# A second norm whose token shift goes through SBUF by DMA, with new instruction orders on all engines

## The chip, the cores and the metric

The kernel runs on one core of a Trainium2 chip. The metric is the device time in microseconds of one execution, as the median of several. TensorE multiplies matrices into PSUM, VectorE and ScalarE work element by element on SBUF and PSUM, GpSimd on SBUF alone, and SyncE (SP) issues the DMAs. Each engine runs its own list of instructions in order; they meet only at semaphores.

## The reference, cut to what matters

`x` is 32 sequences of 128 tokens of 128 features. A cross-attention stage comes first, and then six layers:

```
shift_tokens(t): a, s = halves of the features; s is moved down by one token, the first row is zero
for i in range(6):
    x = attn_layer(shift_tokens(x), ...) + x     # 16 heads of 64, rotary, l2norm of q and k, window 32
    x = ffn_layer(shift_tokens(x), ...) + x
ffn_layer(x): xn = (x - mean) / sqrt(var + 1e-5) * g + b
              a, gate = halves of xn @ W1 + b1 ;  return a * gelu(gate) @ W2 + b2
```

The change is in the second `shift_tokens` of each layer, ahead of the mean and variance of `ffn_layer`. All is float32.

## The kernel before, in words

**Units and rotations.** A unit is one sequence in one layer, 192 in all (`UNITS`). On SBUF a unit's activations are 128 tokens (partitions) by 128 features. The cross-attention (`xslot`, first 340 us) is not touched. After it every engine has a function `slot(n, k)` whose last lines call its parts in a fixed order written out by hand; `slots` (L238) calls it for n from -2 to 196, the middle in a loop of two. In slot n the engine works on several units: z (n+1 or n+2), a (n), m (n-1), b (n-2), c (n-3), d (n-4) and f (n-5). `part(n, lag)` gives the unit, `count` the value that a semaphore has once a unit's step is done. A slot is called a rotation below.

**A unit's way.** The input is copied and transposed (`next_input` L478, `transpose_z` L1272, `copy_z` L649; the first token shift is made by copy_z, which writes half of the rows one column further). a: TensorE makes q and k in four projections `proj_qk(0..3)` and v in two, `proj_v(0..1)`, each 128x512 into bank 0 or 1 in turn; VectorE's `rotary(j)` (two instructions, ta and tb) and ScalarE's `square(j)` read each q/k bank, so that `proj_qk(2)` waits for rotary(0), `proj_qk(3)` for rotary(1), `proj_v(r)` for rotary(r+2); GpSimd's `add(j)` adds ta and tb. `sum_squares` (L967) makes the norms, root(0..3) on VectorE with `log_sum` and `inverse_root` on ScalarE the inverse roots, and GpSimd's `normalize(j)` applies them to unit m. b: `transpose_qk` into banks 4 and 5, `copy_T` out of them, `scores` into banks 2 and 3, `maximum`, `subtract`, `exponent`, `sum_rows`, `invert`, and GpSimd's `weigh`. c: `transpose_P`, `copy_PT`, `attend`, `copy_o`. The values were written to vt by `copy_v` and put into three overlapping windows, vs, by `shift_v` on SP (L317), six DMAs a unit.

**The second norm, unit d.** `attn_out` (L1251) multiplies by Wo into bank 7. `z_mid` (L902) adds the residual and writes zm. `shift_tokens` (L1263) multiplies zm's first half of the features with the identity and its second half with a shift matrix, into bank 6. `norm_stats`, `norm_aggr`, `norm_var` (L911 to L928) take mean and variance from bank 6, GpSimd's `norm_rstd` (L463) the inverse root, and `norm_apply` (L930) reads bank 6 again and writes zn. Then `transpose_zn`, `copy_zn`, `ffn_gate`, `gelu`, `ffn_a`, `gated`. Unit f: `ffn_out` and `z_out` (L894). GpSimd's `residual` (L470) adds b2 to zm for z_out.

**Layer changes.** SP loads the next layer's weights between its shift_v calls (L341 to L362): `load_qk`, `load_v`, `load_o` and `load_ffn` (L298), whose last DMA is b2r. Each waits until the last unit of the layer has used the old weights.

Of the kernel before, what the change touches and what calls it, by code (L numbers as in the profile page):

```python
# [77 lines left out]
def build(nc, x, ctx, deltas, mask, xWq, xWk, xWv, xWo, xtw, Wqkv, qs, ks, Wo, lng, lnb, W1, b1, W2, b2, consts, out):  # L78
    es = ExitStack()
    with es:  # L80
# [6 lines left out]
        def sem(name):  # L87
# [5 lines left out]
        shift = cst[:, C_SH:C_SH + 128]  # L93
# [39 lines left out]
        zm = sb("zm", [128, 2, E])  # L133
# [53 lines left out]
            "l_gb", "l_b2", "l_rot", "l_v0", "l_v1",  # L187
# [7 lines left out]
            "p_zT", "p_qk", "p_v", "p_tr", "p_S", "p_PT", "p_AV", "p_y", "p_zsh", "p_znT", "p_gate", "p_a", "p_y2",  # L195
# [70 lines left out]
        def _(sp):  # L266
# [59 lines left out]

            sp.dma_start(qks[:, 0, :], qs.rearrange("l d -> (l d)").partition_broadcast(128)).then_inc(s["l_qks"], 16)
# [3 lines left out]
            for b in range(B):  # L331
                if b >= 2:

                    sp.wait_ge(s["x_A1"], b - 1)
                sp.dma_start(ctxb[:, b % 2, :], ctx[b, :, :]).then_inc(s[f"l_ctx{b % 2}"], 16)
                if b == 1:
                    load_qk(0)
                    load_v(0)
                    load_o(0)
                    load_ffn(0)  # L340
            for layer in range(DEPTH):  # L341
# [29 lines left out]
        def _(pool):  # L371
# [3 lines left out]
            g.memset(vaug[:, :, :, :], 0.0).then_inc(s["u_vz"], 1)  # L375

# [58 lines left out]
            def slot(n, k):  # L435
# [34 lines left out]
                def residual():  # L470

                    if d_on:
# [3 lines left out]
                        g.tensor_tensor(zmb[:, pd, :], zm[:, pd, :], b2r[:, :], ALU.add).then_inc(s["g_zmb"], 1)  # L476
# [27 lines left out]
                add(3)  # L504
                weigh(1)
# [5 lines left out]
        def _(act):  # L511
# [84 lines left out]
            def slot(n, k):  # L596
# [122 lines left out]
                copy_o(0)  # L719
                copy_o(1)  # L720
# [6 lines left out]
        def _(dve):  # L727
# [123 lines left out]
            def slot(n, k):  # L851
                a, a_on = part(n, 0)
                m, m_on = part(n, 1)
                b, b_on = part(n, 2)
                d, d_on = part(n, 4)
                f, f_on = part(n, 5)
                pm, pb, pd, pf = (k - 1) % 2, k % 2, k % 2, (k - 5) % 2
# [44 lines left out]
                def z_mid():  # L902

                    if d_on:
                        wait(dve, "p_y", count(1, d, 1))
                        wait(dve, "p_zsh", count(1, d - 2, 1))
                        wait(dve, "g_zmb", count(1, d - 2, 1))
                        v_.tensor_tensor(zm[:, pd, :], bank[7][:, 384:512], z_sb[:, cols(d)], ALU.add)\  # L908
# [67 lines left out]
                def sum_rows():  # L976

                    if b_on:
                        wait(dve, "a_exp", count(1, b, 1))
                        v_.tensor_reduce(rs, P[:, pb, :].rearrange("p (h t) -> p h t", t=DH), AX.X, ALU.add)\  # L980
                            .then_inc(s["d_sum"], 1)

                def invert():

                    if b_on:
# [365 lines left out]
```

## Time and profile before

| | |
|---|---|
| median of 3 runs | 3379.66 us (3376.93 to 3380.09) |
| the profiled execution | 3372.05 us, its span 3370.2 us |
| busy: TensorE, VectorE, ScalarE, GpSimd | 3264.7, 2873.8, 2751.3, 2505.5 us |
| granted TensorE clock, mean | 0.991 |
| DMA | 175.94 MB, 52 GB/s |
| longest group of TensorE | the q and k projections, L1149, 1536 matmuls, 806.6 us |
| longest group of GpSimd | add, L452, 768 of 1.28 us each |

A busy time says how long an engine had an instruction in work. Matmuls are pipelined, so that their records overlap by a few tenths; a piece of the chain of waits counts only up to the start of the next. In the rows, PE is TensorE, PEld its load of the stationary operand, DVE is VectorE, ACT ScalarE, POOL GpSimd, SPq the queue of SyncE. Times of a timeline are from the span's start.

### The profile page before, as it was taken

The numbers are of one execution on the slowest core, as the hardware profiler recorded it, in microseconds if no ns is written. First come the engines' busy times: TensorE is split into PE (matmuls) and PEld (weight loads), VectorE is DVE, ScalarE is ACT, GpSimd is POOL, SyncE is SP. The second block draws the span as 40 slices with busy tenths as digits, with TensorE's granted clock in tenths as the row PEclk, the third lists the DMA queues.
The fourth block names the chain that finished last, engine by engine and source line by source line (L and its number), as shares of the span: only waits on it lengthen the run. The fifth ranks groups of instructions, "written<-read, shape, count | busy, mean of one in ns | idle before, by whom it ended". The sixth has DMA issues, their size and how long they took to land.

```text
span 3370.2 us, 170013 instructions
## 1 busy us (share of the span) xinstructions
PE 3264.7 (97%) x65892; PEld 2345.6 (70%) x65892; DVE 2873.8 (85%) x6037; ACT 2751.3 (82%) x5265; POOL 2505.5 (74%) x2703
## 2 busy tenths in 40 slices
PE   6998799999999999999999999999999999999997
PEld 3444477777777777777777777777777777777775
DVE  5888788888888888888888888888888888888885
ACT  3666788888888888888888888888888888888886
POOL 3554677777787777778777787877777787777773
PEclk9999999999999999999999999999999999999998
DMA  2000121112212122221212212122211112221212
GB/s 77 8 7 5 39 57 47 53 50 67 69 47 56 47 55 68 61 55 47 56 47 75 61 49 54 47 56 67 68 48 51 52 47 79 57 56 47 53 50 55
DMA packets 125541, 175.94 MB, mean 52 GB/s; under 512 B 26742, under 2 KB 49332, under 8 KB 124724
## 3 DMA queue, kind: packets, MB, share of 16 engines
q1 hardware_dynamic: 125492, 175.28, 19.4%
q8 instruction: 31, 0.51, 0.1%
q14 instruction: 18, 0.15, 0.0%
HBM read 21.32 MB, written 2.10 MB: 7 GB/s over the span
## 4 chain that ended last, share of the span: by engine, by line
PE 78%; POOL 10%; issue 7%; DMA 1%; DVE 1%; ACT 1%; SPq 1%; POOLq 0%; ACTq 0%; DVEq 0%
PE bank L1149 16%; PE bank L1259 9%; PE bank L1167 9%; PE bank L1159 8%; PE bank L1230 7%; PE bank L1214 6%; POOL qk L452 4%; POOL qk L461 4%; PE bank L1051 3%; PE bank L1293 3%; PE bank L1247 3%; PE bank L1301 3%; PE bank L1268 2%; PE bank L1206 2%; POOL P L490 1%
## 5 line engine op out<-in xcount | busy, mean ns | idle before, releaser
L452 POOL TENSOR_TENSOR qk<-ta,tb 128x512 f32<-128x512 f32 x768 | 982.6, 1280 | 13.0 <-DVE tb L872 13.0
L1149 PE MATMUL bank<-wqkv,zsT 128*128 128x512 f32 x1536 | 806.6, 607 | 6.9 <-ACT zsT L659 2.6
L461 POOL TENSOR_TENSOR qk<-qk,rn 128x512 f32<-128x512 f32 x768 | 795.6, 1048 | 0.0
L610 ACT ACTIVATE sq<-bank 128x512 f32<-128x512 f32 x768 | 461.1, 600 | 322.6 <-PE bank L1149 313.5
L490 POOL TENSOR_TENSOR P<-P,rowsum 128x512 f32<-128x512 f32 x384 | 401.3, 1045 | 375.2 <-DVE rowsum L988 375.2
L869 DVE TENSOR_TENSOR ta<-bank,rot 128x512 f32<-128x512 f32 x768 | 525.8, 685 | 26.7 <-ACT sq L610 11.4
L872 DVE TENSOR_TENSOR tb<-bank,rot 128x512 f32<-128x512 f32 x768 | 521.2, 679 | 0.0
L973 DVE TENSOR_REDUCE bank<-sq 128x32 f32<-128x2048 f32 x192 | 437.8, 2280 | 0.3
L1159 PE MATMUL bank<-wqkv,zsT 128*128 128x512 f32 x768 | 412.3, 619 | 5.4 <-DVE tb L872 5.4
L1259 PE MATMUL bank<-wo,oT 128*128 128x128 f32 x3072 | 393.9, 281 | 0.7 <-ACT oT L636 0.7
L1259 PEld LDWEIGHTS bank<-wo,oT 128*128 128x128 f32 x3072 | 357.3, 191 | 13.8 <-ACT oT L636 1.1
L1167 PEld LDWEIGHTS bank<-cst,qk 64*128 64x128 f32 x6144 | 222.1, 139 | 174.0 <-issue 151.1
L1149 PEld LDWEIGHTS bank<-wqkv,zsT 128*128 128x128 f32 x1536 | 257.2, 198 | 105.9 <-issue 96.3
L1230 PE MATMUL bank<-PT,vs 64*64 64x32 f32 (+1 forms) x18432 | 307.9, 220 | 0.4 <-ACT PT L645 0.4
L1230 PEld LDWEIGHTS bank<-PT,vs 64*64 64x64 f32 x18432 | 286.7, 135 | 30.8 <-issue 30.8
L467 POOL TENSOR_TENSOR rstd<-ve,half_neg 128x1 f32<-128x1 f32 x192 | 105.7, 550 | 263.4 <-DVE ve L928 263.4
L1214 PEld LDWEIGHTS bank<-kT,qT 64*32 64x32 f32 x24576 | 277.4, 105 | 16.2 <-issue 5.9
L1214 PE MATMUL bank<-kT,qT 64*32 64x64 f32 x24576 | 281.0, 225 | 5.3 <-issue 5.3
L908 DVE TENSOR_TENSOR zm<-bank,z_sb 128x128 f32<-128x128 f32 x192 | 56.0, 291 | 263.4 <-PE bank L1259 263.4
L1167 PE MATMUL bank<-cst,qk 64*128 64x64 f32 x6144 | 274.4, 229 | 4.4 <-ACT oT L636 2.5
L620 ACT ACTIVATE qT<-bank 128x512 f32<-128x512 f32 x384 | 229.1, 597 | 47.7 <-PE bank L1167 47.7
L951 DVE TENSOR_TENSOR P<-bank,rowmax 128x512 f32<-128x512 f32 x384 | 260.0, 677 | 0.0
(133 smaller groups left out, 6298.3 us busy)
## 6 DMA issues: line engine op xcount, KB each, us to landing
vs<-vt SPq DMA_DIRECT2D x1152, 128.0 KB, 2.4
wqkv<-L_ffn_Wqkv SPq DMA_DIRECT2D x6, 1024.0 KB, 5.1
wqkv<-L_ffn_Wqkv SPq DMA_DIRECT2D x6, 512.0 KB, 3.8
wo<-L_ffn_Wo SPq DMA_DIRECT2D x6, 512.0 KB, 3.7
z_sb<-x SPq DMA_DIRECT2D x4, 512.0 KB, 6.9
ctxb<-ctx SPq DMA_DIRECT2D x32, 64.0 KB, 1.7
out<-x_sb SPq DMA_DIRECT2D x8, 256.0 KB, 3.5
w<-L_ffn_W SPq DMA_DIRECT2D x6, 341.0 KB, 3.1
```

The source lines that it names most:

```text
L452: g.tensor_tensor(o, i0, i1, ALU.add).then_inc(s["g_add"], 1)
L461: g.tensor_tensor(q3, q3, r3, ALU.mult).then_inc(s["g_qk"], 1)
L610: a_.activation(sq[:, 512 * j:512 * j + 512], bank[j % 2][:, :], ACT.Square)\
L869: v_.tensor_tensor(ta[:, c].rearrange("p (h d) -> p h d", d=DH), bank[j % 2][:, :].rearrange("p (h d) -> p h d", d=DH), rot[:, o:o + 64].u ...
L872: v_.tensor_tensor(tb[:, c].rearrange("p (h c d) -> p h c d", c=2, d=32)[:, :, ::-1, :], bank[j % 2][:, :].rearrange("p (h c d) -> p h c d ...
L973: v_.tensor_reduce(sm, sq[:, :].rearrange("p (h d) -> p h d", d=DH), AX.X, ALU.add)\
L1149: t_.matmul(bank[j % 2][:, :], zsT[:, k % 2, :], wqkv[:, 512 * j:512 * j + 512], start=True, stop=True).then_inc(s["p_qk"], 1)
L1159: t_.matmul(bank[r][:, :], zsT[:, k % 2, :], wv[:, :, r, :], start=True, stop=True)\
L1167: ins = t_.transpose(bank[4 + t][:, 64 * p:64 * p + 64], src[tok, 128 * p:128 * p + 128], ident[tok, tok])
L1214: ins = t_.matmul(SC[e][32 * w:32 * w + 32, 64 * p:64 * p + 64], qT2[dr, p, 32 * w:32 * w + 32], kT2[dr, p, k0:k0 + 64], start=False, stop ...
L1230: ins = t_.matmul(bank[4 + r][64 * e:64 * e + 64, 128 * i + q0:128 * i + q0 + nq], vs[kr, pc, w, hc:hc + 64], PT[kr, 4 * e + i, q0:q0 + nq ...
L1259: ins = t_.matmul(bank[7][:, 384:512], oT[:, p, :], wo[:, 2 * (p % 4) + p // 4, :], start=p == 0, stop=p == PAIRS - 1)
```

## The change

It does four things.

1. `zm` has three parts of 64 features: part 0 the first half, part 2 the second half, part 1 the second half one token later. z_mid writes parts 0 and 2. Row 0 of part 1 is set to zero once by GpSimd.
2. `shift_tokens` on TensorE is gone. SP's new `shift_z` copies part 2 of rows 0 to 126 to part 1 of rows 1 to 127 by one DMA. norm_stats waits for it, and norm_stats and norm_apply read parts 0 and 1 in SBUF. SP issues shift_z(u) ahead of shift_v(u + 3); at a layer change it stands between the loads.
3. sum_rows and invert work on unit n-3 in place of n-2, so that they stand at the start of the next rotation. attend waits for its values itself; values_here is gone.
4. The orders in `slot` of TensorE, VectorE, ScalarE and GpSimd are new.

```diff
-        zm = sb("zm", [128, 2, E])
+        zm = sb("zm", [128, 2, 3, E // 2])
...
@@ SP
+            def shift_z(u, par):
+                wait(sp, "d_zm", count(1, u, 1))
+                sp.dma_start(zm[1:128, par, 1, :], zm[0:127, par, 2, :]).then_inc(s[f"l_s{par}"], 16)
...
                 with sp.Fori(0, (B - 6) // 2) as i:
                     for k in range(2):
+                        shift_z(i * 2 + (start + k), k)
                         shift_v(i * 2 + (start + 3 + k), (3 + k) % 2)
+                shift_z(end - 6, 0)
                 shift_v(end - 3, 1)
+                shift_z(end - 5, 1)
                 if layer + 1 < DEPTH:
                     load_qk(layer + 1)
                 shift_v(end - 2, 0)
                 if layer + 1 < DEPTH:
                     load_v(layer + 1)
+                shift_z(end - 4, 0)
                 shift_v(end - 1, 1)
+                shift_z(end - 3, 1)
                 if layer + 1 < DEPTH:
                     shift_v(end, 0)
+                shift_z(end - 2, 0)
+                if layer + 1 < DEPTH:
                     shift_v(end + 1, 1)
                     load_o(layer + 1)
+                shift_z(end - 1, 1)
+                if layer + 1 < DEPTH:
                     shift_v(end + 2, 0)
                     load_ffn(layer + 1)
@@ GpSimd
+            g.memset(zm[:, :, 1, :], 0.0).then_inc(s["u_s0"], 1)
...
+                next_input()
+                add(0)
                 norm_rstd()
+                normalize(0)
                 residual()
-                add(0)
-                normalize(0)
                 normalize(1)
                 add(1)
+                add(2)
                 normalize(2)
-                next_input()
                 normalize(3)
-                add(2)
                 weigh(0)
+                weigh(1)
                 add(3)
-                weigh(1)
@@ ScalarE
                 square(0)
                 copy_T(0)
+                copy_T(1)
+                square(1)
                 log_sum()
-                copy_T(1)
                 inverse_root()
-                square(1)
                 copy_T(2)
                 copy_T(3)
                 square(2)
-                act.preload_act_table_set("gelu_and_others")
                 copy_z()
                 copy_PT(0)
+                copy_PT(1)
+                square(3)
+                act.preload_act_table_set("gelu_and_others")
                 copy_zn()
-                square(3)
-                copy_PT(1)
+                copy_o(0)
+                copy_o(1)
                 copy_v(0)
                 gelu()
                 act.preload_act_table_set("natural_log_exp_and_others")
                 exponent()
-                copy_o(0)
-                copy_o(1)
                 copy_v(1)
@@ VectorE
                 def norm_stats():
-                        wait(dve, "p_zsh", count(1, d, 1))
-                        v_.bn_stats(stats[:, 0:6], bank[6][:, 0:128]).then_inc(s["d_bn"], 1)
+                        wait(dve, f"l_s{pd}", ...)
+                        v_.bn_stats(stats[:, 0:6], zm[:, pd, 0:2, :].rearrange("p c e -> p (c e)"))
...
-                        v_.tensor_scalar(zn[:, :], bank[6][:, 0:128], mv[:, 0:1], rstd[:, pd:pd + 1],
+                        v_.tensor_scalar(zn[:, :], zm[:, pd, 0:2, :].rearrange("p c e -> p (c e)"), mv[:, 0:1], ...
...
new order: root(0) sum_rows z_mid invert rotary(0) rotary(1) root(1) root(2) root(3) rotary(2)
           norm_stats norm_aggr norm_var z_out maximum(0) norm_apply rotary(3) maximum(1)
           subtract(0) subtract(1) sum_squares gated
@@ TensorE
                 def attend():
-                        pe.wait_ge(s["l_wv"], 16)
+                        wait(pe, f"l_v{pc}", ...)
                         wait(pe, "a_PT", count(2, c, 2))
+                        pe.nop(nofuse=True)
                 def attn_out():
-                        edge(pe, n, "a_gelu", count(1, d - 1, 1))
+                        wait(pe, "a_gelu", count(1, d - 1, 1))
...
                 proj_qk(0)
-                ffn_out()
                 transpose_qk(0)
                 attn_out()
                 proj_qk(1)
                 transpose_qk(1)
-                shift_tokens()
+                ffn_out()
                 proj_qk(2)
                 transpose_z()
+                proj_qk(3)
                 transpose_P()
                 scores()
+                attend()
                 transpose_zn()
-                proj_qk(3)
-                values_here()
                 proj_v(0)
                 ffn_gate()
+                proj_v(1)
                 ffn_a()
-                attend()
-                proj_v(1)
```

## Rows read from the trace of the kernel before

**Rows 1.** The page: busy time, share of the span, instructions; the chain by engine.

```profile
PE 3264.7 (97%) x65892; PEld 2345.6 (70%) x65892; DVE 2873.8 (85%) x6037; ACT 2751.3 (82%) x5265; POOL 2505.5 (74%) x2703
...
PE 78%; POOL 10%; issue 7%; DMA 1%; DVE 1%; ACT 1%; SPq 1%; POOLq 0%; ACTq 0%; DVEq 0%
```

**Rows 2.** The chain of one rotation: start in us, its share in us, what.

```profile
1500.72 0.11 PE bank L1278
1500.83 0.64 PE bank L1167 x16
...
1503.09 0.26 PE bank L1284
1503.35 0.86 PE bank L1149 x2
...
1506.39 1.53 PE bank L1230 x96
1507.93 1.05 PE bank L1159 x2
...
1509.84 0.67 PE bank L1247 x6
...
1514.64 0.36 PE bank L1268 x2
...
1515.23 0.98 PE bank L1149 x2
```

**Rows 3.** The chain from 860 to 1360 us: two starts of attn_out, 11 rotations apart.

```profile
937.68 1.98 PE bank L1259 x16
...
1107.80 1.98 PE bank L1259 x16
```

**Rows 4.** Timeline of VectorE: start, us, instruction, idle before it and its releaser.

```profile
1514.35 0.68 DVE L872 TENSOR_TENSOR tb<-bank,rot 128x512 f32<-128x512 f32 x1
...
1517.28 0.40 DVE L935 TENSOR_SCALAR zn<-bank,mv,rstd 128x128 f32<-128x128 f32 x1
1517.59 0.68 DVE L869 TENSOR_TENSOR ta<-bank,rot 128x512 f32<-128x512 f32 x1
...
1518.79 1.28 DVE L942 TENSOR_REDUCE rowmax<-bank 128x8 f32<-128x512 f32 x2
...
1525.35 1.21 DVE L980 TENSOR_REDUCE bank<-P 128x16 f32<-128x1024 f32 x1
...
1527.01 0.19 DVE L882 TENSOR_SCALAR bank<-bank 128x32 f32<-128x32 f32 x1
1528.86 0.29 DVE L908 TENSOR_TENSOR zm<-bank,z_sb 128x128 f32<-128x128 f32 x1 [1.67 <-PE bank L1259]
1529.19 0.69 DVE L869 TENSOR_TENSOR ta<-bank,rot 128x512 f32<-128x512 f32 x1
```

**Rows 5.** Norm instructions from SBUF, cross-attention part; last, norm_rstd later; durations ns min/median/max.

```profile
L842 DVE TENSOR_SCALAR z_sb<-x1cur,mv,rstd x32: 346/1051/1056, 62.3 to 340.0; 128x128 f32 x26, 128x128 f32<-128x128 f32 x6
...
199.42 1.04 POOL L416 TENSOR_TENSOR qk<-qk,xmax 128x512 f32<-128x512 f32 x1
199.49 1.05 DVE L842 TENSOR_SCALAR z_sb<-x1cur,mv,rstd 128x128 f32 x1 [0.30 <-POOL rstd L428]
...
207.25 0.28 DVE L825 BATCH_NORM_STATS2 stats<-x1cur 128x6 f32<-128x128 f32 x1
...
1516.12 0.55 POOL L467 TENSOR_TENSOR rstd<-ve,half_neg 128x1 f32<-128x1 f32 x1 [1.38 <-DVE ve L928]
```

**Rows 6.** shift_v's DMAs, 860 to 1360 us: issue in ns, landing, min/median/max.

```profile
L325 SPq DMA_DIRECT2D vs<-vt x193: 461/597/614, 859.8 to 1356.0; - x193
...
DMA to landing us min/median/max: 2.2/2.4/2.5
```

**Rows 7.** Timeline of SP at a layer change: first and last DMA of load_ffn.

```profile
891.47 0.53 SPq L304 DMA_DIRECT2D gb<-L_ffn_ln_g  x1
...
896.82 0.34 SPq L315 DMA_DIRECT2D b2r<-L_ffn_b  x1
```

More of the change, by code:

```diff
@@ L475, in residual @@
                         wait(pool, "z_ready", count(1, d - 2, 1) + B if not (isinstance(d, int) and d < 2) else 0)
-                        g.tensor_tensor(zmb[:, pd, :], zm[:, pd, :], b2r[:, :], ALU.add).then_inc(s["g_zmb"], 1)
+                        g.tensor_tensor(zmb[:, pd, :].rearrange("p (c e) -> p c e", c=2), zm[:, pd, 0:3:2, :],
+                                        b2r[:, :].rearrange("p (c e) -> p c e", c=2), ALU.add)\
+                            .then_inc(s["g_zmb"], 1)
                 def next_input():
@@ L854, in slot @@
                 b, b_on = part(n, 2)
+                c, c_on = part(n, 3)
                 d, d_on = part(n, 4)
                 f, f_on = part(n, 5)
-                pm, pb, pd, pf = (k - 1) % 2, k % 2, k % 2, (k - 5) % 2
+                pm, pb, pc, pd, pf = (k - 1) % 2, k % 2, (k - 3) % 2, k % 2, (k - 5) % 2
                 ym, sm, n0, n1, rs = rn[:, pm, :], SC[0][:, 0:32], SC[0][:, 32:64], SC[0][:, 64:96], SC[1][:, 0:16]
@@ L905, in z_mid @@
                         wait(dve, "p_y", count(1, d, 1))
-                        wait(dve, "p_zsh", count(1, d - 2, 1))
                         wait(dve, "g_zmb", count(1, d - 2, 1))
-                        v_.tensor_tensor(zm[:, pd, :], bank[7][:, 384:512], z_sb[:, cols(d)], ALU.add)\
+                        v_.tensor_tensor(zm[:, pd, 0:3:2, :], bank[7][:, 384:512].rearrange("p (c e) -> p c e", c=2),
+                                         z_sb[:, cols(d)].rearrange("p (c e) -> p c e", c=2), ALU.add)\
                             .then_inc(s["d_zm"], 1)
@@ L913, in norm_stats @@
                     if d_on:
-                        wait(dve, "p_zsh", count(1, d, 1))
-                        v_.bn_stats(stats[:, 0:6], bank[6][:, 0:128]).then_inc(s["d_bn"], 1)
+                        wait(dve, f"l_s{pd}", 16 * (d // 2) + 16 if isinstance(d, int) else (d >> 1) * 16 + 16)
+                        v_.bn_stats(stats[:, 0:6], zm[:, pd, 0:2, :].rearrange("p c e -> p (c e)"))\
+                            .then_inc(s["d_bn"], 1)
                 def norm_aggr():
@@ L976, in sum_rows @@
                 def sum_rows():
-                    if b_on:
-                        wait(dve, "a_exp", count(1, b, 1))
-                        v_.tensor_reduce(rs, P[:, pb, :].rearrange("p (h t) -> p h t", t=DH), AX.X, ALU.add)\
+                    if c_on:
+                        wait(dve, "a_exp", count(1, c, 1))
+                        v_.tensor_reduce(rs, P[:, pc, :].rearrange("p (h t) -> p h t", t=DH), AX.X, ALU.add)\
                             .then_inc(s["d_sum"], 1)
                 def invert():
-                    if b_on:
-                        wait(dve, "d_sum", count(1, b, 1))
-                        wait(dve, "g_P", count(2, b - 1, 2))
+                    if c_on:
+                        wait(dve, "d_sum", count(1, c, 1))
+                        wait(dve, "g_P", count(2, c - 1, 2))
                         v_.reciprocal(rowsum[:, :], rs).then_inc(s["d_rec"], 1)
-                z_out()
-                root(0)
-                z_mid()
-                rotary(0)
-                root(1)
-                norm_stats()
-                root(2)
-                norm_aggr()
-                root(3)
-                norm_var()
-                rotary(1)
+                root(0)
+                sum_rows()
+                z_mid()
+                invert()
+                rotary(0)
+                rotary(1)
+                root(1)
+                root(2)
+                root(3)
+                rotary(2)
+                norm_stats()
+                norm_aggr()
+                norm_var()
+                z_out()
+                maximum(0)
                 norm_apply()
-                rotary(2)
-                maximum(0)
+                rotary(3)
                 maximum(1)
                 subtract(0)
-                rotary(3)
                 subtract(1)
+                sum_squares()
                 gated()
-                sum_squares()
-                sum_rows()
-                invert()
             slots(dve, slot)
@@ L1221, in attend @@
                     if c_on:
-                        pe.wait_ge(s["l_wv"], 16)
+                        wait(pe, f"l_v{pc}", 96 * (c // 2) + 96 if isinstance(c, int) else (c >> 1) * 96 + 96)
                         wait(pe, "a_PT", count(2, c, 2))
+                        pe.nop(nofuse=True)
                         for i in range(4):
@@ L1234, in attend @@
                                 ins.then_inc(s["p_AV"], 1)
-                def values_here():
-                    if c_on:
-                        wait(pe, f"l_v{pc}", 96 * (c // 2) + 96 if isinstance(c, int) else (c >> 1) * 96 + 96)
                 def ffn_out():
@@ L1261, in attn_out @@
                         ins.then_inc(s["p_y"], 1)
-                def shift_tokens():
-                    if d_on:
-                        wait(pe, "d_zm", count(1, d, 1))
-                        wait(pe, "z_ready", (count(1, f, 1) if isinstance(f, int) else d) + B)
-                        t_.matmul(bank[6][:, 0:64], ident, zm[:, pd, 0:64], start=True, stop=True)
-                        t_.matmul(bank[6][:, 64:128], shift, zm[:, pd, 64:128], start=True, stop=True)\
-                            .then_inc(s["p_zsh"], 1)
                 def transpose_z():
```

8 lines of the change are left out of this document (5 added, 3 removed).

## The prediction

> **What bounds the kernel now.** I read the page's busy times first, then the chain that ended last, then one rotation of that chain piece by piece, then the timeline of the other engines over the same rotation. TensorE is busy for 97% of the span, VectorE for 85%, and TensorE holds 78% of the chain [rows 1]. The word "rotation" below is one call of `slot`: one unit enters and the engines work on units n to n-5. In the steady part the chain is TensorE without a break: the 11 rotations between the two starts of attn_out take 170.12 us, so one takes 15.465 us [rows 3]. Its pieces are one 512-column projection at 0.86 us, a group of 16 transposes at 0.64, attend at 1.53, and so on [rows 2]. VectorE sat idle for 1.67 us in that rotation, just ahead of z_mid, which waits for attn_out [rows 4]. So work taken from TensorE pays until another loop closes at its own length; how much pays is the question.
>
> **What goes from TensorE.** The two matmuls of shift_tokens hold the chain from 1514.64 to 1515.23, 0.59 us [rows 2]. The order also drops one change of operand shape from 64-row groups to 128 rows. What such a change costs: proj_v(1) behind attend takes 1.05 against 0.86 (0.19) and proj_qk(2) behind the shift 0.98 against 0.86, which is partly its wait for rotary(0) [rows 2]. In the new order proj_v(1) and proj_qk(2) have 128-row work ahead of them (-0.19, -0.12), ffn_out gets such a change in their place (+0.17, my value between 0 and 0.19), and transpose_zn keeps its 0.26 behind attend in place of the scores. TensorE alone would come to 15.465 - 0.59 - 0.19 - 0.12 + 0.17 = 14.74 us.
>
> **The loop that closes first.** z_mid now is followed by invert, rotary(0) and rotary(1), and proj_qk(3) waits for rotary(1), since it takes bank 1 (`d_rot` of j - 1). Counted from z_mid's start: z_mid to the next operation 0.33, invert about 0.17 (as the short operations, 0.19 long and overlapping), rotary(0) 1.20 by the distance of two VectorE operations around a rotary, then rotary(1)'s second half ends 0.60 + 0.68 later: 2.98 us [rows 4]. From the end of a rotary's second half (1514.35 + 0.68 = 1515.03) to the end of the projection that waited for it (1515.23 + 0.98 = 1516.21) is 1.18 us [rows 2, 4]. So proj_qk(3) ends 4.16 us after z_mid starts. z_mid starts about 0.23 behind attn_out's end, an estimate somewhat under the 0.32 that the hand-over from VectorE to TensorE costs (1.18 - 0.86); I use it again for maximum(0) behind the scores. In the same time TensorE has only proj_qk(1) 0.86, transpose_qk(1) 0.64, ffn_out 0.84, proj_qk(2) 0.86, transpose_z 0.11, proj_qk(3) 0.86 = 4.17 us of work [rows 2] where the path by VectorE takes 4.39: TensorE stalls by 0.2 in each rotation. That makes 14.74 + 0.22 = 14.96 us.
>
> VectorE has a loop of the same length. Behind proj_qk(3): transpose_P 0.64, masks and scores 1.62 (from the end of the transposes at 1501.47 to 1503.09), 0.23 of latency [rows 2]: maximum(0) starts 6.65 us after z_mid. From there to sum_rows VectorE does what it did before from norm_apply to sum_rows (1517.28 to 1525.35, 8.07 us), less rotary(2) (1.20) and with root(0) (0.17): 7.04; sum_rows 1.21; and z_mid again [rows 4]. That is 14.90 us, and about 0.1 for subtract(1), whose whole 0.68 the sum of squares must now await where gated() stood between: 15.0 us. VectorE's own work fits in (its idle time is now ahead of maximum(0), 0.6 to 0.9 us). ScalarE's work is unchanged: 82% of 15.465 is 12.7 us [rows 1], which leaves it over 2 us of 15.0. I cost its new order at nothing; what it could delay is transpose_qk(1), which needs banks 4 and 5 back from copy_T(1), and each tenth by which copy_T(1) were late there would be a tenth per rotation. GpSimd has the same instructions as before; weigh waits for invert, which is behind z_mid now, but transpose_P has 3.5 us more of TensorE work ahead of it than the two weighs' 2.1 (two of 1.04 us, the form and length of [rows 5]).
>
> **The transfer.** shift_z is one DMA per unit, waited for three rotaries and three roots later. Between z_mid's end and norm_stats lie invert, 3 x 1.20 and the dependent roots, some 4.5 us. No transfer of this shape (127 partitions of 256 bytes, inside SBUF) is in the trace. The nearest, vs<-vt inside SBUF, lands 2.2 to 2.5 us after its issue, and an issue holds SP for 0.46 to 0.61 us [rows 6]. Bounds: 2.2 and, with an issue ahead of it, 3.1; I take 2.4 and so nothing in the steady rotations. SP has the six issues of shift_v behind it, not ahead of it: 7 x 0.65 = 4.6 us of a rotation.
>
> **norm_stats and norm_apply read SBUF now.** bn_stats from SBUF took 0.28 in the cross-attention part against 0.30 from PSUM: nothing [rows 5]. The tensor_scalar is another matter. From PSUM it took 0.40 [rows 4]. The same operation from SBUF to SBUF took 1.05 us when a GpSimd tensor_tensor had begun 0.07 us before it, ending 0.08 us after that one (199.42 + 1.04 and 199.49 + 1.05), and 0.346 at the shortest of 32 [rows 5]. So the price is from -0.05 to +0.65 us per rotation, somewhat more behind a longer GpSimd instruction. It depends on the phase. GpSimd's norm_rstd waits for norm_var (it did so before, 1.38 us [rows 5]), so normalize(0) starts about 0.6 us after it, near 6.4 us (statistics from 4.9, the three dependent steps 0.9), and holds until 7.4; norm_apply comes at 6.65 + 0.60 = 7.25. It would end near 7.6, as from PSUM. I take +0.1 for the spread: 15.1 us per rotation.
>
> The Trainium skill (SBUF — State Buffer, on the shared port pair) says that a VectorE instruction in a 2-port mode and a GpSimd instruction take an exclusive lock: the later one "fully blocks". The trace's 1.05 us row agrees with it. By that rule the sum is 15.0 or 15.65 us a rotation, as the phase has it; that is the second rival below.
>
> **Layer changes.** load_ffn(layer + 1) stands ahead of the next layer's first shift_z on SP. It begins when gated() of the last unit is done, about 13.7 us after z_mid, and its issues took 5.35 us up to b2r's [rows 7]. So shift_z of the new layer's first unit is issued about 19.6 us after the z_mid before (z_mid's own time is 15.1), lands at 22.0 to 22.3, where norm_stats would stand at 19.9. Of the 2.2 us the idle time ahead of maximum(0) takes 0.6: 1.7 us at each of 5 changes, +9 us (bounds 0 and 15). Before, a late b2r held only GpSimd there.
>
> **The tail.** In the last rotations nothing covers the transfer: 2.4 and an issue's 0.5 in place of TensorE's 0.59 and its hand-over of 0.3, about +2 us in each of three, +6.
>
> **Sum.** About 188 full rotations x (15.1 - 15.465) = -68.6; +9; +6: -54 us. The profiled execution took 3372.05 us (span 3370.2, 1.85 around it): 3318. The median of the runs shown is 7.6 above that execution, so about 3326.
>
> **The rivals.**
> 1. TensorE stays the only bound, the latencies that I added between engines being too long by 0.2 us. For it: its chain had no gap before. Against: the loop by rotary(1) is two rows long and not a guess. 188 x (14.74 - 15.465) = -136, +15: 3258 in this state of the count. 16%.
> 2. The other side: norm_apply is caught by a GpSimd instruction in most rotations. Place: VectorE's loop, which has nothing to give between maximum(0) and z_mid, and transpose_zn, which waits for it with 0.3 us in hand. Price 0.65: 15.0 + 0.65 = 15.65, 188 x 0.185 = +35, +15: 3430. It turns the change into a loss from 0.39 us per rotation on (15.465 - 15.0 - 15/188 = 0.385). For it: with a median of 1.051 over 32 at least half were caught there [rows 5], and GpSimd is busy 74% of the span [rows 1]. Against: the phase above. 14%.
> 3. The transfer lands behind norm_stats' place, because shift_v's issues get ahead of it: 3.9 us of issues, 6.3 us, 1.8 late, of which 0.7 is idle time anyway: +1.1 on 15.1 for all rotations, 3326 + 207 = 3533. Against: the order on SP, where both values' semaphores are up before z_mid's. 4%.
> 4. One engine's new order makes a loop of about the old length (a copy_T(1) that transpose_qk(1) awaits, an exponent that sum_rows awaits: both have 0.1 to 0.3 us in hand) and nothing moves: 3380. 6%.
>
> **Chances.** The forecast has 60%, with 3290 to 3360 as its own range (0.2 us of a rotation is 38 us). About 0.2% is what a measurement of this kernel can tell from no change. Faster: the 60 and 16, and 1 from the mild form of the second: 0.77. Same: 4's 6%, 0.06. Slower: 13 of the second and 4 of the third, 0.17. The range reaches to the first rival's value, 3258, and over the mild half of the second: 3258 to 3405.
>
> **What would show it.** A distance of attn_out's starts of 15.0 to 15.2 us. Idle time of TensorE's weight load for rotary(1) ahead of proj_qk(3), 0.1 to 0.3 us in each rotation. zn's tensor_scalar at 0.35 to 0.7 us; at 1.0 and above the second rival holds. No VectorE wait for the DMA in steady rotations and one of 1.5 to 3 us at each of 5 layer changes. Distances of 14.7 would show the first rival; a wait for zm's DMA in all rotations the third; 15.4 or more without either the fourth.

## The result: 0.5% faster, a third of the gain forecast, and the profile after

| | before | after |
|---|---|---|
| median of 7 runs | 3379.66 us (3371.06 to 3381.19) | 3360.43 us (3353.22 to 3364.67) |
| ratio | | 0.9947, 95% interval 0.9935 to 0.9958 |
| profiled execution, its span | 3372.05, 3370.2 us | 3357.84, 3356.0 us |
| one rotation, mean of 16 (distance of z_mid's starts) | 15.466 us | 15.186 us |

The forecast was 3326 us, -54; measured are -19 between the medians and -14.2 between the two spans. The page's busy times and its chain by engine, after, beside [rows 1]:

```profile
PE 3232.1 (96%) x65124; PEld 2208.1 (66%) x65124; DVE 2921.4 (87%) x6037; ACT 2673.6 (80%) x5265; POOL 2501.8 (75%) x2704
...
PE 90%; issue 3%; DVE 3%; DMA 1%; POOL 1%; ACT 1%; SPq 1%; DVEq 0%; ACTq 0%; POOLq 0%
```

TensorE is busy 32.6 us less. What that bought is seen in the chain of one rotation (start, share in us, what), which answers to [rows 2]; L1170 is proj_qk, L1188 a group of transposes, L1264 ffn_out, L1286 transpose_z, L1180 proj_v, L1301 ffn_gate, L1309 ffn_a, L1276 attn_out:

```profile
1509.21 0.65 PE bank L1188 x16
1509.85 0.86 PE bank L1264 x6
1510.72 1.00 PE bank L1170 x2
1511.72 0.11 PE bank L1286
1511.83 1.09 PE bank L1170 x2
...
1517.84 0.79 PE bank L1301 x6
1518.63 0.86 PE bank L1180 x2
1519.49 0.66 PE bank L1309 x6
```

The matmuls of the shift and the dearer proj_v are gone. But proj_qk(2) takes 1.00 and proj_qk(3) 1.09 where 0.86 is the work, and ffn_gate 0.79 where the like-sized ffn_a takes 0.66: TensorE waits in three places. VectorE and SP over the same rotation, from the timeline (start, us, instruction, idle before it and its releaser), beside [rows 4]:

```profile
1508.74 0.29 DVE L927 TENSOR_TENSOR zm<-bank,z_sb 128x128 f32<-128x128 f32 x1 [0.47 <-PE bank L1276]
1509.06 0.64 SPq L329 DMA_DIRECT2D zm<-zm  x1
...
1511.05 0.68 DVE L892 TENSOR_TENSOR tb<-bank,rot 128x512 f32<-128x512 f32 x1
...
1513.68 0.28 DVE L935 BATCH_NORM_STATS2 stats<-zm 128x6 f32<-128x128 f32 x1
```

z_mid still waits for attn_out (0.47 us), and proj_qk(3) begins as rotary(1)'s second half ends (1511.05 + 0.68 = 1511.73): that is the loop of the forecast. The statistics need no wait for the transfer in this rotation.

Cut at z_mid's starts, the 14.2 us come out as follows. 191 rotations at -0.280 make -53.5. Five things give a part of it back. The first z_mid starts 2.6 us later (398.16 against 395.53). The first four rotations stood 1.8 us above the mean before and stand 6.6 above it after: 4.8. The twelve rotations around each of the five layer changes stood 6.4 us above the mean in all and stand 24.2 above: 17.8. The last six were 7.6 us under the mean and are 4.2 over it: 11.7. Behind the last z_mid 22.0 us follow in place of 19.8: 2.2. The sum is -14.4.

The first of the five is not the change's. The cross-attention stage, which is the same in both kernels, already ran 5.0 us late at its first norm and 5.7 at its last in this one execution of the changed kernel; the line of [rows 5] reads 62.3 to 340.0 before and here:

```profile
L861 DVE TENSOR_SCALAR z_sb<-x1cur,mv,rstd x32: 347/1051/1056, 67.3 to 345.7; 128x128 f32 x26, 128x128 f32<-128x128 f32 x6
```

In the profiled executions of the experiments its last norm starts anywhere from 339.2 to 351.0. From there to the first z_mid the changed kernel takes 52.5 us, the kernel before 55.5. Without this scatter the two spans differ by 20 us, as the medians do.

### The profile page after: what moved, and what is told of

It reads as the page before. It is cut to its first block, busy times and chain, and to the rows that moved or that the text cites. A ratio compares the mean times of both kernels' runs of the same rounds, so it can differ in the third digit from the quotient of the medians.

```text
span 3356.0 us, 168541 instructions
## 1 busy us (share of the span) xinstructions
PE 3232.1 (96%) x65124; PEld 2208.1 (66%) x65124; DVE 2921.4 (87%) x6037; ACT 2673.6 (80%) x5265; POOL 2501.8 (75%) x2704
## 2 busy tenths in 40 slices
DMA packets 150118, 182.19 MB, mean 54 GB/s; under 512 B 51318, under 2 KB 73908, under 8 KB 149300
## 4 chain that ended last, share of the span: by engine, by line
PE 90%; issue 3%; DVE 3%; DMA 1%; POOL 1%; ACT 1%; SPq 1%; DVEq 0%; ACTq 0%; POOLq 0%
PE bank L1170 20%; PE bank L1276 11%; PE bank L1188 10%; PE bank L1180 9%; PE bank L1252 8%; PE bank L1235 7%; PE bank L1264 5%; PE bank L1301 4%; PE bank L1309 4%; PE bank L1072 3%; PE bank L1227 2%; PE bank L1292 1%; PE bank L1089 1%; DMA zm<-zm 1%; PE bank L1286 1%
## 5 line engine op out<-in xcount | busy, mean ns | idle before, releaser
L469 POOL TENSOR_TENSOR qk<-ta,tb 128x512 f32<-128x512 f32 x768 | 969.0, 1273 | 10.4 <-DVE tb L892 10.4
L1170 PE MATMUL bank<-wqkv,zsT 128*128 128x512 f32 x1536 | 818.8, 615 | 4.9 <-DVE tb L892 2.2
L509 POOL TENSOR_TENSOR P<-P,rowsum 128x512 f32<-128x512 f32 x384 | 392.4, 1042 | 514.8 <-DVE rowsum L1009 514.8
L1188 PEld LDWEIGHTS bank<-cst,qk 64*128 64x128 f32 x6144 | 221.8, 139 | 291.5 <-issue 291.5
L1180 PE MATMUL bank<-wqkv,zsT 128*128 128x512 f32 x768 | 400.5, 604 | 2.4 <-DVE tb L892 2.3
L1276 PE MATMUL bank<-wo,oT 128*128 128x128 f32 x3072 | 395.4, 282 | 0.5 <-ACT gl L709 0.5
L1276 PEld LDWEIGHTS bank<-wo,oT 128*128 128x128 f32 x3072 | 358.9, 192 | 13.8 <-issue 0.9
L963 DVE TENSOR_REDUCE rowmax<-bank 128x8 f32<-128x512 f32 x384 | 263.1, 685 | 93.2 <-PE bank L1235 93.1
L664 ACT ACTIVATE PT<-bank 128x512 f32<-128x512 f32 x384 | 208.4, 595 | 159.1 <-PE bank L1188 159.1
L1170 PEld LDWEIGHTS bank<-wqkv,zsT 128*128 128x128 f32 x1536 | 232.3, 191 | 110.9 <-DVE tb L892 98.0
L1188 PE MATMUL bank<-cst,qk 64*128 64x64 f32 x6144 | 274.3, 229 | 2.5 <-issue 2.1
## 6 DMA issues: line engine op xcount, KB each, us to landing
zm<-zm SPq DMA_DIRECT2D x192, 31.8 KB
```

Source lines behind the costliest of these rows:

```text
L469: g.tensor_tensor(o, i0, i1, ALU.add).then_inc(s["g_add"], 1)
L1170: t_.matmul(bank[j % 2][:, :], zsT[:, k % 2, :], wqkv[:, 512 * j:512 * j + 512], start=True, stop=True).then_inc(s["p_qk"], 1)
L1180: t_.matmul(bank[r][:, :], zsT[:, k % 2, :], wv[:, :, r, :], start=True, stop=True)\
L1188: ins = t_.transpose(bank[4 + t][:, 64 * p:64 * p + 64], src[tok, 128 * p:128 * p + 128], ident[tok, tok])
L1276: ins = t_.matmul(bank[7][:, 384:512], oT[:, p, :], wo[:, 2 * (p % 4) + p // 4, :], start=p == 0, stop=p == PAIRS - 1)
```

## Experiments

Ratios are to the kernel before, timed in the same batches. "Rotation" is the mean of 16; "changes" the excess over the mean of the five layer changes. Diffs are against the changed kernel, that of e9 against e5, those of e10 and e11 against e9.

| kernel | edit | ratio, 95% | rotation | changes |
|---|---|---|---|---|
| after | | 0.9947, 0.9935 to 0.9958 | 15.186 | 24.2 |
| e3 | new orders, shift on TensorE | 0.9966, 0.9949 to 0.9982 | 15.367 | 0.3 |
| e1 | SP's order | 0.9884, 0.9859 to 0.9909 | 15.189 | 1.0 |
| e2 | invert ahead of z_mid | 0.9932, 0.9908 to 0.9955 | 15.166 | 30.2 |
| e4 | ffn_gate later | 0.9963, 0.9947 to 0.9979 | 15.213 | |
| e7 | rotary(0), invert ahead of z_mid | 0.9942, 0.9927 to 0.9958 | 15.183 | |
| e5 | e7 and e1 | 0.9890, 0.9870 to 0.9909 | 15.192 | 8.9 |
| e8 | old orders, transfer | 1.1443, 1.1422 to 1.1464 | 17.834 | |
| e6 | GpSimd's phase | 0.9991, 0.9979 to 1.0004 | 15.244 | |
| e9 | e5, GpSimd waits for norm_apply | 0.9747, 0.9723 to 0.9771 | 14.927 | 9.1 |
| e10 | e9, z_mid earlier | 0.9756, 0.9732 to 0.9781 | 14.929 | |
| e11 | e9, another tail | 0.9776, 0.9753 to 0.9798 | 14.93 | |

**e3: the orders without the transfer.** The shift is back on TensorE, between ffn_out and proj_qk(2).

```diff
-        zm = sb("zm", [128, 2, 3, E // 2])
+        zm = sb("zm", [128, 2, E])
...
                 ffn_out()
+                shift_tokens()
                 proj_qk(2)
```

> The new orders on all engines, with the second norm's token shift back on TensorE (two matmul groups between ffn_out and proj_qk(2)) and no transfer of zm. Theory A (a rotation closes by z_mid, invert, rotary(0), rotary(1), proj_qk(3) and TensorE's chain behind it): the shift puts 0.59 us into the stretch of TensorE between attn_out and proj_qk(3), which has 0.2 to 0.35 us to give, so a rotation is 14.9 (TensorE alone with its wait for copy_zn) + 0.6 = 15.5 us; the layer changes, the start and the tail lose nothing to a transfer: about 3375 us, ratio 0.995 to 1.005, so the orders alone bring nothing. Theory B (VectorE with its 90% busy time is the bound, TensorE only follows): a rotation stays at 15.19 and the time falls to about 3325 us, ratio 0.984.

The orders alone bring 15.466 to 15.367, the transfer the next 0.18. The chain of e3; L1265 and L1266 are the two groups of the shift, L1150 proj_qk(2) and (3):

```profile
1521.08 0.17 PE bank L1265 x2
1521.25 0.22 PE bank L1266 x2
1521.47 0.91 PE bank L1150 x2
...
1522.50 0.86 PE bank L1150 x2
```

Behind 128-row work the shift costs 0.39 us, not the 0.59 of [rows 2], and proj_qk(3) does not wait. So the transfer takes 0.39 off TensorE and gives 0.21 of it back as waits. It also owns the layer changes (0.3 us here against 24.2): over 191 rotations its 0.18 is 34 us, and the changes eat 24 of them. I had expected 15.5 us and no gain from the orders, with the shift at 0.59. The last six rotations take 95.49 us here, 95.30 after and 85.24 before. The lost tail therefore belongs to the orders.

**e1: SP's order.** shift_z(end - 1) goes ahead of load_o and the new layer's first shift_z ahead of load_ffn.

```diff
-                shift_z(i * 2 + (start + k), k)
                 shift_v(i * 2 + (start + 3 + k), (3 + k) % 2)
+                shift_z(i * 2 + (start + 1 + k), (1 + k) % 2)
...
-                    load_o(layer + 1)
                 shift_z(end - 1, 1)
                 if layer + 1 < DEPTH:
+                    load_o(layer + 1)
                     shift_v(end + 2, 0)
+                    shift_z(end, 0)
                     load_ffn(layer + 1)
```

> The changed kernel with another order on SP at the layer changes alone: shift_z(end - 1) ahead of load_o, and shift_z of the next layer's first unit ahead of load_ffn. Theory A (the uncovered transfers of zm cost 3.3 to 5.5 us at each of 5 layer changes, since they queue behind wo's 512 KB and behind load_ffn's twelve issues): the rotation at a layer change falls from 18.3 to 20.7 us to 15.2 to 16 us, all others stay at 15.12 and 15.26, and the time falls by 17 to 24 us, to about 3340, ratio 0.987 to 0.990. Rival (the loss there is from the weights' own arrival, b2r and w1, as it was before the change): less than 5 us, since these DMAs now come 1 us later.

The excess of 24.2 falls to 1.0 and the ratio by 0.0063, 21 us, with the same rotation. The loss at the changes is thereby shown to be SP's order. In the timeline of the changed kernel at one change, the transfer of the layer's last unit is issued behind the 512 KB of wo, and that of the next unit behind load_ffn's issues:

```profile
875.25 0.39 SPq L295 DMA_DIRECT2D wo<-L_ffn_Wo  x1
875.76 0.66 SPq L329 DMA_DIRECT2D zm<-zm  x1
...
880.93 0.29 DVE L935 BATCH_NORM_STATS2 stats<-zm 128x6 f32<-128x128 f32 x1 [0.52 <-DMA zm<-zm]
...
890.85 0.29 DVE L927 TENSOR_TENSOR zm<-bank,z_sb 128x128 f32<-128x128 f32 x1
...
895.38 0.67 SPq L329 DMA_DIRECT2D zm<-zm  x1
...
899.40 0.29 DVE L935 BATCH_NORM_STATS2 stats<-zm 128x6 f32<-128x128 f32 x1 [3.53 <-DMA zm<-zm]
```

The first transfer is a piece of 5.14 us in the chain. The second is issued 4.2 us after its z_mid has ended, and the statistics wait 3.53. e1 moved both at once; the distances of z_mid's starts part them. In the rotation of the first transfer they are 15.26 to 15.42 us at the five changes, 15.26 in e1; in that of the second 18.33 to 20.68, against 15.12. So nearly all is lost behind load_ffn. The first adds to it by making gated, and with it load_ffn, 0.3 to 0.6 us later.

More is lost there than the wait. norm_apply, now in the time of a GpSimd instruction, takes 0.81 us, and TensorE stands 2.7 to 3.5 us without work ahead of transpose_zn. At four of the five changes its granted clock fell in this idle time or just behind it from 1.00, the upper level (2.4 GHz), to 0.50, the lower one (1.2 GHz), for some 3 to 7 us, and one or both proj_v took up to twice their time. At the change near 1882 us the clock stayed at 1.00 behind a like idle time (2.90). The first three lines are TensorE's idle time (timeline), its clock (a stretch of 2 us, third figure from the end) and proj_v(1) (chain) at the first change; the last is proj_v(1) near 1882 us:

```profile
901.94 0.33 PE L1292 MATMUL bank<-cst,zn 128*128 128x128 f32 x1 [2.91 <-DVE zn L956]
904.00:906.00 2.00, 2.00 (x5) 0.97 (x4) 1.87 (x3) 1.98 (x5) 2.00 (x3) 0.50 0.04 12
904.35 1.71 PE bank L1180 x2
...
1886.51 0.86 PE bank L1180 x2
```

The rotation with the clock at 1.00 throughout took 18.33 us, the four others 19.84 to 20.68: 1.5 to 2.4 us more, some 7 of the 24 us in all. That is an estimate, since the waits differ too (3.2 to 4.1).

In e1 the issues stand the other way round, and the statistics start without a wait. A late arrival of the new weights, the other reading of the change's cost, is thereby refuted: they are issued later in e1, behind the transfer.

```profile
893.64 0.66 SPq L329 DMA_DIRECT2D zm<-zm  x1
894.40 0.79 SPq L303 DMA_DIRECT2D gb<-L_ffn_ln_g  x1
...
898.26 0.28 DVE L936 BATCH_NORM_STATS2 stats<-zm 128x6 f32<-128x128 f32 x1
```

**e2: invert ahead of z_mid.**

```diff
                 sum_rows()
-                z_mid()
                 invert()
+                z_mid()
                 rotary(0)
```

> The changed kernel with invert ahead of z_mid on VectorE, where VectorE has 0.3 to 0.5 us of idle time, in place of behind it. Theory A (the path by z_mid, invert, rotary(0) and rotary(1) holds proj_qk(3)): the path shortens by 0.18 us, a rotation comes to 15.0 to 15.05 us, TensorE's wait for rotary(1) nearly goes, and the time falls by some 30 us to 3330, ratio 0.985. Theory B (VectorE's own work is the bound): the same instructions, no change, 0.9947. Theory C (TensorE with its wait ahead of ffn_gate is the bound already): no change either, and its wait ahead of proj_qk(3) turns into another.

It should shorten the loop by rotary(1), and the rotation moves by 0.02. VectorE's timeline in e2 shows why:

```profile
1511.36 1.21 DVE L1001 TENSOR_REDUCE bank<-P 128x16 f32<-128x1024 f32 x1
1512.73 0.26 DVE L1009 RECIPROCAL rowsum<-bank 128x16 f32<-128x16 f32 x1 [0.15 <-DVE bank L1001]
1513.13 0.29 DVE L927 TENSOR_TENSOR zm<-bank,z_sb 128x128 f32<-128x128 f32 x1
```

Right behind its source the reciprocal starts 1.37 us after sum_rows, z_mid 0.40 after that, and z_mid has no wait for attn_out left: VectorE's own chain has taken over at nearly the same length.

**e4: ffn_gate behind proj_v(1)**, to cover its wait for copy_zn.

```diff
                 proj_v(0)
-                ffn_gate()
                 proj_v(1)
+                ffn_gate()
```

> The changed kernel with proj_v(1) ahead of ffn_gate on TensorE. In the changed kernel ffn_gate's first matmul group takes 0.79 us of the chain in place of 0.66, since only proj_v(0) stands between transpose_zn and it while copy_zn runs. Theory A: those 0.13 us per rotation go, a rotation is 15.05 us, the time falls by 20 to 25 us, ratio 0.988. Rival (gelu and with it the exponent come 0.4 us later on ScalarE, so that sum_rows and z_mid on VectorE wait): 0 to 0.1 us per rotation worse, ratio 0.995 to 1.0.

Nothing is gained (15.213, 0.03 more). In e4's chain the wait reappears as a piece without work ahead of transpose_qk(1), which needs the banks of copy_T(1):

```profile
1506.10 0.32 issue
1506.42 0.71 PE bank L1188 x16
```

ScalarE's copy_T(0) and copy_T(1) run from 1505.23 to 1506.32 there, ending 0.1 us ahead of that group: with gelu later, ScalarE works without a pause from gelu to copy_T(1), and its loop closes at about the old length.

**e7 and e5: rotary(0) first.** e7 takes z_mid out of the path to rotary(1); e5 adds e1's edit.

```diff
                 sum_rows()
-                z_mid()
-                invert()
                 rotary(0)
+                invert()
+                z_mid()
                 rotary(1)
```

> The changed kernel with VectorE's order root(0), sum_rows, rotary(0), invert, z_mid, rotary(1) in place of root(0), sum_rows, z_mid, invert, rotary(0), rotary(1). Rotary(0) then fills the time in which VectorE waits for attn_out, and only rotary(1) stands behind z_mid. Theory A' (invert's move brought nothing because a reciprocal right behind its reduction stalls and z_mid then starts late by VectorE; proj_qk(3) does wait for rotary(1)): rotary(1) ends some 0.4 to 0.5 us sooner, TensorE's 0.2 to 0.4 us ahead of proj_qk(2) and proj_qk(3) go, a rotation comes to 14.9 to 15.0 us, about 3315 us, ratio 0.982. Theory C (TensorE's own chain is at its end in the changed kernel, whatever VectorE does): 15.15 to 15.19, no change. Risk: one rotary less covers the transfer; it lands 3.1 us after z_mid's end at a place that now is 3.3 to 3.7 us behind it.

> The same VectorE order together with the SP order that was tried by itself (shift_z(end - 1) ahead of load_o, the next layer's first shift_z ahead of load_ffn). Theory A': the two gains add, since they lie in different rotations: about 3295 us, ratio 0.976. If VectorE's order brings nothing: 3340, 0.988.

The rotation stays at 15.18. The timeline of e7:

```profile
1505.51 0.29 DVE L935 BATCH_NORM_STATS2 stats<-zm 128x6 f32<-128x128 f32 x1 [0.31 <-DMA zm<-zm]
...
1506.94 1.04 POOL L478 TENSOR_TENSOR qk<-qk,rn 128x512 f32<-128x512 f32 x1
1507.19 0.87 DVE L956 TENSOR_SCALAR zn<-zm,mv,rstd 128x128 f32<-128x128 f32 x1
1508.12 0.33 PE L1292 MATMUL bank<-cst,zn 128*128 128x128 f32 x1 [0.16 <-DVE zn L956]
```

z_mid no longer waits for attn_out; it starts 1.6 us behind it. The loop is now VectorE's own, through the transfer: VectorE waits for the landing (0.31), and between the statistics and the next z_mid it never stands idle for longer than 0.13. In that stretch lies norm_apply, which begins inside GpSimd's normalize(0), ends 0.08 us after it, takes 0.87 us in place of 0.34, and now makes TensorE wait. Both are terms of this loop; e9 takes out the second.

**e8: the transfer alone**, in the old orders.

> The kernel before with only the token shift by the transfer inside SBUF (zm's three parts, shift_z on SP, no shift_tokens on TensorE), all orders on TensorE, VectorE, ScalarE and GpSimd as before. Between z_mid and norm_stats lie only rotary(0) and root(1), 1.5 us, and the transfer needs about 3: VectorE waits some 1.6 us in every rotation. Theory A (TensorE waits for rotary(1), which is behind norm_stats here): a rotation grows to 15.8 to 16.3 us, 3440 to 3540 us, ratio 1.02 to 1.05. Rival (the wait only takes the place of VectorE's idle time ahead of z_mid, 1.0 to 1.7 us a rotation): no change or the 0.4 us gained from TensorE, ratio 0.98 to 1.0.

The ratio was far above the 1.02 to 1.05 that I expected: the price is 2.37 us per rotation. Its timeline:

```profile
1510.03 0.29 DVE L926 TENSOR_TENSOR zm<-bank,z_sb 128x128 f32<-128x128 f32 x1 [0.52 <-PE bank L1279]
1510.35 0.64 SPq L329 DMA_DIRECT2D zm<-zm  x1
...
1514.05 0.29 DVE L934 BATCH_NORM_STATS2 stats<-zm 128x6 f32<-128x128 f32 x1 [2.25 <-DMA zm<-zm]
...
1516.06 1.12 DVE L955 TENSOR_SCALAR zn<-zm,mv,rstd 128x128 f32<-128x128 f32 x1
```

VectorE stands 2.25 us for the transfer, and norm_apply takes 1.12 us where it took 0.40 [rows 4]. The transfer is issued 0.03 us after z_mid's end, so nothing on SP holds it up. The three rotaries and three roots that the new orders put between are a condition of the transfer.

**e6: GpSimd's phase.** residual ahead of normalize(0).

```diff
                 norm_rstd()
-                normalize(0)
                 residual()
+                normalize(0)
```

> The changed kernel with residual ahead of normalize(0) on GpSimd, both behind norm_rstd. normalize(0) then starts 0.4 us later, still runs when norm_apply comes, and ends 0.4 us later. Theory A (the two-port read of zm waits until the GpSimd instruction that holds the port is done, so only the phase made it cheap): norm_apply takes 0.7 to 0.8 us in the steady rotations in place of 0.34, and as VectorE has only 0.3 to 0.5 us to give ahead of z_mid, a rotation grows by 0 to 0.15 us, ratio 0.995 to 1.002. Rival (0.34 is what this instruction takes beside GpSimd in any phase): 0.34, and 0.9947.

All norm_apply of the changed kernel, of e6, of e7 and of e9, one line each (ns min/median/max):

```profile
L956 DVE TENSOR_SCALAR zn<-zm,mv,rstd x192: 336/339/934, 405.0 to 3339.4; 128x128 f32<-128x128 f32 x192
```

```profile
L956 DVE TENSOR_SCALAR zn<-zm,mv,rstd x192: 336/733/1241, 397.9 to 3344.1; 128x128 f32<-128x128 f32 x192
```

```profile
L956 DVE TENSOR_SCALAR zn<-zm,mv,rstd x192: 403/880/1437, 399.0 to 3335.0; 128x128 f32<-128x128 f32 x192
```

```profile
L959 DVE TENSOR_SCALAR zn<-zm,mv,rstd x192: 335/338/470, 399.2 to 3270.1; 128x128 f32<-128x128 f32 x192
```

Moving a small GpSimd instruction takes it from 0.34 to 0.73 us, and the rotation grows by 0.06; the other 0.3 us were in hand. So the second rival's mechanism is real; in the changed kernel the phase avoids it. The Trainium skill (SBUF — State Buffer, Who interferes with whom) says that the later of the two is fully blocked. e6 and e7 agree: in e6 normalize(0) starts at 1510.21 and takes 1.05 us, norm_apply starts at 1510.59 and ends at 1511.34, 0.1 behind it, as in e7.

**e9: e5, and GpSimd's normalize(0) waits for norm_apply.**

```diff
                         wait(pool, "g_add", count(4, m, j + 1))
+                        if j == 0 and d_on:
+                            wait(pool, "d_zn", count(1, d, 1))
```

> The kernel with rotary(0) ahead of z_mid and the two shift_z ahead of the weights' loads, plus one wait: GpSimd's normalize(0) waits for d_zn, so that norm_apply reads zm with GpSimd quiet. In the run without that wait norm_apply took 0.87 us and TensorE waited 0.16 us for it in each rotation. Theory A'' (what held the rotation at 15.19 there was norm_apply behind normalize(0), 0.53 us on VectorE's chain, in place of the path by rotary(1)): norm_apply 0.34 us, a rotation of 14.9 to 15.0 us, about 3290 to 3300 us, ratio 0.976 to 0.978. Rival (the transfer of zm, awaited 0.3 us in each rotation there, or TensorE's own chain holds it): 15.1 to 15.19, ratio 0.986 to 0.989. GpSimd has 3.0 us of idle time per rotation for the wait.

This is the fastest kernel: 0.9747, 3288.55 us. Against e5 the rotation falls by 0.265 us; over 191 rotations that is 51 us, and the ratios differ by 0.0143, 48 us. Every norm_apply now runs free, and e9's chain has proj_qk(2) and proj_qk(3) at 0.86 (L1173), with ffn_gate's wait alone left (L1304):

```profile
1508.48 0.86 PE bank L1173 x2
...
1509.45 0.86 PE bank L1173 x2
...
1515.23 0.80 PE bank L1304 x6
```

GpSimd pays for it where hardly anybody waits. In the waits of 1000 to 3300 us (sum, count, longest) it idles 145.9 us for norm_apply, 1 us a rotation:

```profile
POOL qk L481 <- DVE zn L959: 145.9, 149, 2.7
```

At the layer changes 9 us stay in e5 and e9 where e1 has 1.0. GpSimd's residual waits for b2r there, up to 4.4 us; that this is the cause was not tried.

**e10: e9 with z_mid ahead of invert**, 0.2 us earlier against attn_out.

```diff
                 rotary(0)
-                invert()
                 z_mid()
+                invert()
                 rotary(1)
```

> The same with z_mid ahead of invert behind rotary(0), which issues the transfer 0.17 us sooner and weigh later. If the wait for the transfer holds the rotation: 0.1 to 0.17 us less per rotation, 20 to 30 us less than the kernel with invert first. If TensorE's chain or another loop does: the same within 0.2%.

The same within the interval (14.929). In e9 the landing is no longer a bound: TensorE's own chain is. In e7 and e5 it is another matter. The statistics waited for it in about 140 of 151 rotations there, in 8 in e9. That the lock on norm_apply held them is shown by e9; whether an earlier landing would have helped them as well was not tried.

**e11: another tail.** In the last five rotations of e9, TensorE puts attend behind ffn_a, where it stood in the kernel before, and leaves out the projections, which have no unit left; ScalarE puts gelu and exponent ahead of copy_o.

```diff
+                if isinstance(n, int) and n >= UNITS:
...
+                    scores()
+                    transpose_zn()
+                    ffn_gate()
+                    ffn_a()
+                    attend()
...
```

> The fastest kernel so far (rotary(0) first, shift_z ahead of the weights, normalize(0) awaiting d_zn) with the order of before in the last five rotations alone (n from UNITS on) on TensorE and ScalarE: attend behind ffn_a in place of ahead of transpose_zn, and gelu and exponent ahead of copy_o. Theory T (the tail's loss of 11 to 12 us in the changed kernel is from the orders, since attend stands ahead of transpose_zn there and with no projections to hide it the norm's chain waits for it; the kernel with the orders alone and no transfer lost 11 of them too): 4 to 10 us less in the last six rotations, about 3282 us, ratio 0.972 to 0.9735. Rival (the tail's loss is the uncovered transfer, 3.5 to 3.7 us a unit): the last six rotations as long as before, no change.

The last six rotations take 98.94 us against 94.53 in e9. My reading of the tail fell. By e3 its loss lies in the orders; which of them stays open.

## Why the prediction was wrong: the loop named rightly, four terms too small

Of the 39 us between the forecast's -54 and the -14 of the two spans, 15 lie in the steady rotations, 9 at the layer changes, 7 at the start (5.7 of them the scatter told above, -3.1 and +4.8 the change's) and 8 in the tail.

**The steady rotation** was forecast at 15.1 and measured at 15.186, a fall of 0.280 where 0.365 was forecast. The loop that closes first is the one named: z_mid, rotary(0), rotary(1), proj_qk(3), with a stall of 0.23 and 0.16 in two rotations running where 0.2 was forecast. The waits of the changed kernel from 1000 to 3300 us (about 151 rotations; sum, count, longest) say the same, and name the other two places:

```profile
PEld bank L1170 <- DVE tb L892: 72.1, 149, 0.5
PEld bank L1301 <- ACT znT L686: 103.2, 150, 0.8
...
DVE rowmax L963 <- PE bank L1235: 70.9, 144, 2.0
...
DVE stats L935 <- DMA zm<-zm: 18.3, 9, 4.1
```

VectorE's idle time ahead of maximum(0), 0.49 a rotation, was forecast at 0.6 to 0.9. The statistics waited for the transfer in 9 rotations, no steady cost.

**TensorE alone** was put at 14.74. e9 runs on its own chain at 14.93, and 14.80 without the 0.13 of ffn_gate. That wait is the term I left out, and the step that failed here: I cost ScalarE's new order at nothing. In the new order only proj_v(0) stands between transpose_zn and the gate, where proj_qk(3) and proj_v(0) stood before, and ffn_gate waits for ScalarE's copy_zn. The pieces add up: 14.80 + 0.13 + 0.07 (proj_qk(2), 0.14 in every other rotation) + 0.20 (proj_qk(3)) = 15.20, against 15.186. e3 as well: 14.80 + 0.13 + 0.39 + 0.05 (proj_qk(2), 0.91) = 15.37, against 15.367. The 0.12 on proj_qk(2) did not come as forecast: rotary(0), behind z_mid now, is late for it in every other rotation.

**The phase argument** was right: 0.339 us at the median, within the bound of -0.05 below 0.40. My allowance of 0.1 for it was not needed. That it nearly made up for the missing 0.13 was luck. By this rotation the gain is 191 x 0.280 = 53.5 us where the forecast had 68.6: 15 of the 39 us that are missing.

**The transfer** was mis-sized. I took 2.4 us, at most 3.1. From the issue to the start of the statistics it takes 3.7 us, in e7 and e8 as well. At the end of the changed kernel nothing covers it:

```profile
3333.98 0.29 DVE L927 TENSOR_TENSOR zm<-bank,z_sb 128x128 f32<-128x128 f32 x1 [2.60 <-PE bank L1276]
...
3337.95 0.29 DVE L935 BATCH_NORM_STATS2 stats<-zm 128x6 f32<-128x128 f32 x1 [3.68 <-DMA zm<-zm]
```

In a steady rotation 4.65 us lie between z_mid's end and the statistics (1509.03 to 1513.68), so it stays hidden all the same.

**The layer changes** were forecast at +9 and measured at +17.8, and e1 takes nearly all of it away. The issue was placed rightly: shift_z of the new layer's first unit goes out 19.6 to 19.9 us after the z_mid before, where I had 19.6. What failed is what follows. The transfer is used 3.9 to 4.6 us after its issue, not 2.4, so that VectorE waits 3.2 to 4.1 us where I had 2.2. The slower norm_apply (0.81) and TensorE's lower clock behind its idle time had no term at all. load_o ahead of shift_z(end - 1) was not counted either; it cost little.

**Start and tail.** Forecast 0 and +6, measured +7.4 (1.7 without the scatter) and +13.9. I asked only what the transfer does there. e3 has the same tail without one, so the pipeline's filling and draining under the new orders was the missing term: with sum_rows and attend in another place, the last units meet another wait in each rotation. That this is the mechanism is argued; e11 shows only that one repair of it is none. A part is the clock again: over the last six rotations it was granted at 0.98 before, 0.89 after and 0.91 in e3, and TensorE was busy 75.3, 78.4 and 79.3 us there.

**The rivals.** The first (14.74) was wrong in the changed kernel and nearly right for e9. The second did not hold, but its mechanism was in the next bound: without it e5 falls from 15.19 to 14.93. The third did not hold; e8 has its sign, a wait for the transfer in each rotation, from another cause, the missing cover. The fourth appeared in e2 and e4: several loops lie within 0.3 us, and shortening one alone bought 0.02 at most.

## What to carry to other kernels

When several loops through different engines are of nearly one length, remove them in the order in which they close and look for the next before judging an edit: e7's order was worth nothing until one wait on an engine with time to spare freed the VectorE instruction that GpSimd blocked (0.26 us a rotation). A small transfer put on a shared queue must be followed past every other load on it, above all at the rare places where weights change, and a wait there has to be followed into TensorE, whose clock can fall behind it. And a new order is to be walked through the pipeline's first and last rotations too, where its covers are missing.

## What was not expected of the hardware

- A transfer inside SBUF of 127 rows of 256 bytes (31.8 KB) takes 3.7 us from its issue to the start of the instruction that waited; one of 128 KB in rows of 2 KB lands after 2.2 to 2.5 us [rows 6]. The two ends are not the same, and which property of the transfer costs the time was not tried. Packets under 512 bytes are 51318 on the page of the changed kernel, 26742 before.
- The same two matmul groups cost 0.59 us where TensorE came from 64-row work [rows 2] and 0.39 behind 128-row work (e3).
- Behind 2.7 to 3.5 us without work TensorE ran at half its clock for some 3 to 7 us at four of the five layer changes, and at full clock at the fifth; a projection of v took up to 1.71 us in place of 0.86.
